# The sixth addition of out products moved into the first reciprocal-square-root chain of each transition, in an eight-stage transformer kernel

## What is computed

```python
x = x + L0_xattn(layernorm(x), ctx)     # stage 0
x = x + L0_ffn(layernorm(x))            # stage 1
x = x + L1_xattn(layernorm(x), ctx)     # stage 2
x = x + L1_ffn(layernorm(x))            # stage 3
x = x + L2_xattn(layernorm(x), ctx)     # stage 4
x = x + L2_ffn(layernorm(x))            # stage 5, mixture of experts
x = x + L3_xattn(layernorm(x), ctx)     # stage 6
x = x + L3_ffn(layernorm(x))            # stage 7

def layernorm(x, eps=1e-5):
    m = mean(x); v = var(x)             # over the 512 features
    return (x - m) / sqrt(v + eps)
```

## Time and profile before

| what | value |
|---|---|
| median of 3 runs | 3057.5 us |
| lowest, highest run | 3056.55, 3062.46 us |
| the profiled execution's own time | 3064.65 us |
| its span in the profile | 3062.8 us |
| mean granted TensorE clock | 0.986 of full |
| DVE / ACT / POOL busy | 1709.6 / 1122.2 / 986.7 us |

### The profile page before, as it was taken

The page is one execution under the profiler, slowest core; times in us unless marked ns, Lnnn a source line. Parts: engine busy times, 40 slices in busy tenths (PEclk is TensorE's granted clock), DMA queues, the critical chain, the costliest instruction groups (busy, mean ns, idle before and its releaser), DMA issues.

```text
span 3062.8 us, 47964 instructions
## 1 busy us (share of the span) xinstructions
PE 2935.8 (96%) x16224; PEld 2493.0 (81%) x16224; DVE 1709.6 (56%) x3508; ACT 1122.2 (37%) x3631; POOL 986.7 (32%) x836
## 2 busy tenths in 40 slices
PE   7999999999999989899989999999889999999899
PEld 6888888888878867688778888888768888888687
DVE  6554445454453258778666666666654455444644
ACT  4222223222242246732354444444423333333432
POOL 3333333334222246433332223332223333332221
PEclk9999999999999999899999999999999999999999
DMA  3111111111111010011111011110011111110111
GB/s 121 41 48 40 44 33 40 47 40 47 36 42 56 27 42 29 27 35 34 39 39 29 28 31 34 34 34 18 25 43 45 39 34 34 34 34 21 45 46 48
DMA packets 68565, 119.75 MB, mean 39 GB/s; under 512 B 8681, under 2 KB 14185, under 8 KB 68065
## 3 DMA queue, kind: packets, MB, share of 16 engines
q1 hardware_dynamic: 68450, 118.26, 12.7%
HBM read 116.06 MB, written 2.10 MB: 39 GB/s over the span
## 4 chain that ended last, share of the span: by engine, by line
PE 86%; DVE 8%; issue 3%; ACT 3%; POOL 1%; DMA 0%; DVEq 0%; SPq 0%; POOLq 0%; ACTq 0%
PE proj L390 39%; PE outp L390 23%; PE heado L965 6%; PE score L929 5%; PE turn L952 2%; PE score L390 2%; PE score L1473 1%; PE outp L1894 1%; PE proj L406 1%; DVE pbuf L1189 1%; DVE acts L1276 1%; PE heado L1894 1%; ACT acts L1110 1%; DVE x L1710 0%; PE proj L895 0%
## 5 line engine op out<-in xcount | busy, mean ns | idle before, releaser
L390 PE MATMUL outp<-w_out,acts 128*128 128x512 f32 x3288 | 843.0, 401 | 17.8 <-DVE x L1250 6.9
L390 PE MATMUL proj<-xnT,w_in 128*128 128x512 f32 x3192 | 762.4, 394 | 4.8 <-DVE big L1032 2.5
L390 PEld LDWEIGHTS outp<-w_out,acts 128*128 128x128 f32 x3288 | 597.1, 189 | 145.5 <-DVE x L496 11.2
L390 PEld LDWEIGHTS proj<-xnT,w_in 128*128 128x128 f32 x3192 | 596.8, 189 | 131.4 <-DVE big L1032 2.9
L390 PE MATMUL proj<-ctxT,w_kv 128*128 128x512 f32 x1536 | 367.8, 396 | 18.7 <-POOL w_kv L700 18.7
L698 POOL TENSOR_TENSOR w_out<-ring,consts 128x512 fp32r<-128x512 f32 x96 | 102.1, 1063 | 827.7 <-PE outp L390 827.7
L390 PEld LDWEIGHTS proj<-ctxT,w_kv 128*128 128x128 f32 x1536 | 288.4, 190 | 78.2 <-issue 18.7
L1250 DVE TENSOR_TENSOR x<-x,outp 128x512 f32<-128x512 f32 x360 | 245.2, 685 | 185.3 <-PE outp L390 182.2
L1032 DVE COPY big<-proj 128x512 f32<-128x512 f32 x136 | 93.6, 688 | 341.2 <-PE proj L390 338.6
L1029 ACT ACTIVATE big<-proj 128x512 f32<-128x512 f32 x136 | 81.4, 599 | 487.1 <-PE proj L390 480.7
L698 POOL TENSOR_TENSOR w_kv<-ring,consts 128x512 fp32r<-128x512 f32 x93 | 97.1, 1044 | 459.3 <-DMA ring<-in_L_wk 440.0
(11 more groups left out here) (319 smaller groups left out, 4121.6 us busy)
## 6 DMA issues: line engine op xcount, KB each, us to landing
ring<-in_L_wq SPq DMA_DIRECT2D x96, 256.0 KB, 2.7
ring<-in_L_wo SPq DMA_DIRECT2D x96, 256.0 KB, 2.7
ring<-in_F_in SPq DMA_DIRECT2D x52, 256.0 KB, 2.6
ring<-in_L_wk SPq DMA_DIRECT2D x48, 256.0 KB, 2.7
ring<-in_L_wv SPq DMA_DIRECT2D x48, 256.0 KB, 3.2
ring<-in_F_out SPq DMA_DIRECT2D x41, 256.0 KB, 2.6
x<-in_x SPq DMA_DIRECT2D x2, 1024.0 KB, 8.4
big<-in_ctxT SPq DMA_DIRECT2D x4, 512.0 KB, 8.1
```

The costliest lines, as they stand in the source:

```text
L390: mm = pe.matmul(bank_ap, w_ap(a, c), rhs(b, c), start=first and c == 0 and n == 0, stop=last and c == chunks - 1 and n == len(PASSES) - 1)
```

## The change

`dve_ln_rstd` takes `between` and hands it to `dve_rsqrt`; `dve_tail` gives it addition 5 for the first chain, and the loop behind the chain begins at addition 6.

```diff
-        def dve_ln_rstd(dve, n, half, arg=None, work=None):
+        def dve_ln_rstd(dve, n, half, arg=None, work=None, between=None):
...
-            dve_rsqrt(dve, rstd[:, cols], arg, work, ln_shifted, ln_newton, ln_calls[0])
+            dve_rsqrt(dve, rstd[:, cols], arg, work, ln_shifted, ln_newton, ln_calls[0], between)
...
-            dve_ln_rstd(dve, n, 0)
-            for b in range(BH + 1, B):
+            dve_ln_rstd(dve, n, 0, between=lambda: add_of(BH + 1))
+            for b in range(BH + 2, B):
                 add_of(b)
             dve_ln_rstd(dve, n, 1)
             dve_ln_norm(dve, n, 4)
```

## The result

The changed kernel took a median of 3063.36 us (20 runs, 3056.36 to 3073.4) against 3057.97 us of the kernel before in the same job (20 runs, 3053.09 to 3062.46). The ratio is 1.0015 with a 95% interval of 1.0008 to 1.0021: slower by 4.6 us (the two medians lie 5.4 us apart). The forecast was 3057.9, in a range that ended at 3062.0.

A forecast was written before the change was run, and what follows sets the result against it. PE was taken to bound the kernel, with ACT's work nearly the whole path after the first chain in short transitions. Terms 1.64 + 0 - 1.26 = +0.4 us on the 3057.5 us median gave 3057.9 us, range 3054 to 3062.

The forecast's parts named there:

- The four alike transitions: Entries to stages 1, 4, 5 and 7: second chain and K projection 0.41 us later each, +1.64 us together.
- stage 3: Entry to stage 3: ACT's vanished wait offsets the first chain's loss, 0 us, between 0 and +0.41.
- stage 6: Entry to stage 6: addition 5 and product 7 start earlier, -1.26 us, the chain's loss hidden in ACT's idle time.
- if the clock came back: Rival, product 7 at stage 6 at full clock: up to -3.31 us there, 3055.8 us in all; chance 0.25.
- ACT without a pause ahead of deviation 7: Sign of being right, four short entries: ACT's 0.23 us idle time before deviation 7 disappears.
- additions' waits: Sign of being right: PE's out-product waits for additions fall from 14.5 us to about 8.
- the wait at stage 6: Sign of being right, entry to stage 6: PE idle about 4.3 us instead of 5.58.
- the clock of the four short transitions: Entries to stages 1, 4, 5 and 7: the forecast sum included no clock change there.
- the rival of low stretches: Longer PE pauses bring new 1.2 GHz stretches behind transitions: +7.2 us, 3064.7 us; chance 0.07.
- the pause ahead of batch 2: PE's pause between transposes of batches 1 and 2: claimed to grow as norm 2 comes 0.41 us later.
- a clock under 1.00 into stage 5: Sign of being wrong, entry to stage 5: clock below its present 1.00 would mean the clock has the larger say.
- four new stretches of 1.7 us: Low-clock stretches behind transitions needed for a slower verdict: 0.4 + 4 x 1.7 = +7.2 us; three give 5.5.

The follow-up runs named there:

- b_same: The kernel before, unchanged, run beside itself: mean 3060.3 us over 11 executions, ratio 1.0005.
- only_14: Kernel before with addition 5 moved at the entries to stages 1 and 4 alone: mean 3065.8 us, ratio 1.0011.
- only_14_b: Repeat run of the kernel with addition 5 moved at the entries to stages 1 and 4 alone: mean 3066.2 us, ratio 1.0020.
- short_only: Kernel before with addition 5 moved at the entries to stages 1, 4, 5 and 7 alone: mean 3063.3 us, ratio 1.0010.
- all of before: The 138 executions of the unchanged kernel in the jobs of the follow-up experiments: mean 3060.1 us, mean clock 0.9881.

## Why the prediction was wrong

- *The path.* The mechanism was right. The four alike transitions cost 0.40 us each (0.41 forecast), stage 3 gained 0.06 (0 forecast, and within its spread), and stage 6 was mis-sized: it gained 2.26 (1.26 forecast, with 3.31 as the end if the clock came back). Product 7 was taken to run at the low clock for all of its 5.37 us; the clock came back during it, and it took 4.35. Sum -0.7 instead of +0.4, so the path alone had the wrong sign, and both are small. At equal clock the change is worth about -1 us.
- *Where the waits go.* Right: ACT without a pause ahead of deviation 7, additions' waits from 14.5 to 7.6 us (8 forecast), the wait at stage 6 4.33 us (4.3).
- *The clock.* This step failed. The sum took the clock of the four short transitions as unchanged, a term of 0, and the rival of low stretches was given 0.07. Over all executions the mean clock fell by 0.0015 to 0.0016, which is worth about +3.6 us, more than the whole path. In the profiles it is found at stages 5 and 7, 3.1 us together. The place was named rightly, the pause ahead of batch 2, and so was the sign that a clock under 1.00 into stage 5 would give the clock the larger say (0.86, 0.72, 0.72 in three profiles). I asked for four new stretches of 1.7 us and thought them too many; about two are what came. That three of the four entries had a low stretch already was held against the rival, from one profile. Other executions of the same kernel have none at stage 7 (1.00 in b_same, only_14 and only_14_b), so there was one to lose; with the new order no unfilled profile is at 1.00 there. That the stretch at stage 7 grows as well (0.72 to 0.58) cost nothing.
- *The range.* It was built on three runs. The mean of 138 executions of the kernel before is 3060.1 us, 2.6 above the median of those three, so the middle itself stood too low. The allowance of 0.2%, or 6.1 us, for what a measurement can tell was wide too: 20 executions of each told 4.6 us. What is left of those 4.6 us beyond the 2.6 of all executions is no part of any term; the first job's executions of before were 1.6 us shorter on average than the 138 later ones.
- *The rule of the Trainium skill* by which DVE copies between matmuls leave PE warm (TensorE: Matmul & The Clock Gate, Loop structure matters more than you think) would have put the loss at 0; short_only lost 3.2 us against all of before, with a clock of 0.9865 against 0.9881. Another section of that page of the Trainium skill, A second HAM failure mode: psum-queue depth-cycling, says that short idle times between groups of matmuls can make the clock go to and fro; that agrees with these runs, where no pause of PE listed above for the four entries was longer than 2.2 us and the clock of the changed kernel was lower all the same.

## What to carry to other kernels

When a wait of TensorE is moved rather than removed, look at where the pauses stand afterwards: two short pauses with a product between them may keep the clock, the same idle time in one sparse stretch may not, and the later work pays. Compare executions at equal granted clock to part the path from the clock, but trust it to a few us only, since a low stretch costs by what PE does in it; the time of a stage between two fixed instructions, beside its clock, says what a stretch cost. One profile of each kernel told the wrong sign here. Work without use in a pause, short enough to end before the awaited input, is a test of the clock and here won more than the change that was studied, though not in every filling.

## What was not expected of the hardware

- Ten transposes of 1.25 us at four places, which delayed nothing in the trace, made a kernel of 3060 us faster by 3.0 us, and by 7.3 in the other order; with more of them the kernel before fell to 3052.7 us.
- A stage can stay at 1.2 GHz while PE is busy: 27.2 of 28 us at a granted clock of 0.51 in only_14_b, with matmuls of 136 columns. The stage took 62.15 us instead of 52.06.
- A longer low stretch need not cost more: at stage 7 a window at 0.58 and one at 0.72 were followed by an end at the same distance (192.7 and 192.4 us), one at 1.00 by an end 2.4 us nearer.
- Two edits at different transitions do not add up: entries 5 and 7 cost 3.8 and 6.7 us (two runs), entries 1 and 4 cost 5.6 and 6.0, the four together 3.2 (short_only; all against all of before).
